# Stacking 85 inner rows in two weight tiles, direct copies across halves, and gram moves issued by GpSimd

## The reference, cut to what matters

```python
# N_DENSE 13, N_FIELDS 26, VOCAB 6250, K 64, batch 512, HID = 325 + 26*64 + 13 = 2002
sparse_embed = emb_tables[field_idx[None, :], x_sparse]          # 512 x 26 x 64, gathered rows
z = sparse_embed.reshape(B, N_FIELDS * K)
gram = jnp.einsum('bik,bjk->bij', sparse_embed, sparse_embed)
inner = gram[:, iu, ju]                                          # the 325 pairs i < j
dnn_in = jnp.concatenate([x_dense, z, inner], axis=-1)           # 512 x 2002
h = jax.nn.relu(dnn_in @ w1 + b1)                                # w1 is 2002 x 2002
out = jax.nn.sigmoid(h @ w2 + b2)
```

## Time and profile before

| | |
|---|---|
| median of 3 runs | 210.6 us (209.88 to 210.68) |
| profiled execution, its own time | 210.68 us |
| its span, first to last instruction | 208.6 us |
| PE busy | 200.1 us (96%) |
| DVE, ACT, POOL busy | 145.3, 130.2, 121.2 us |
| moved by DMA | 38.99 MB, 187 GB/s on average |

### The profile page before, as it was taken

One profiled execution on the slowest core, in us unless ns is written; L12 is line 12 of the kernel. 1 busy time (PEld: TensorE's weight loads), 2 busy tenths in 40 slices (PEclk: granted clock), 3 DMA queues, 4 the chain that ended last, 5 costly groups with the idle time before them and its releaser, 6 DMA issues.

```text
span 208.6 us, 3830 instructions
## 1 busy us (share of the span) xinstructions
PE 200.1 (96%) x1340; PEld 163.9 (79%) x1340; DVE 145.3 (70%) x341; ACT 130.2 (62%) x262; POOL 121.2 (58%) x162
## 2 busy tenths in 40 slices
PE   8999989989999969999999999999999999999993
PEld 8966868868888848878888888888888888788882
DVE  3656829088879289678587989557498896673473
ACT  2755437089989578889367663868689957542201
POOL 4878777778777781446898898889883000000000
PEclk9999999999999996999999999999999999999999
DMA  5389958788785922266787648768868385023100
GB/s 152 95 268 290 306 219 279 300 281 282 257 262 187 291 55 23 102 154 161 217 281 229 205 119 294 247 217 257 292 209 231 91 279 212 3 46 55 32 0 0
DMA packets 15387, 38.99 MB, mean 187 GB/s; under 512 B 3881, under 2 KB 5281, under 8 KB 15369
## 3 DMA queue, kind: packets, MB, share of 16 engines
q1 hardware_dynamic: 11688, 35.27, 52.1%
q0 software_dynamic: 3328, 3.41, 7.2%
q10 hardware_dynamic: 353, 0.08, 0.2%
HBM read 37.71 MB, written 0.69 MB: 184 GB/s over the span
## 4 chain that ended last, share of the span: by engine, by line
PE 60%; POOL 21%; issue 7%; DMA 6%; ACT 2%; DVE 2%; DVEq 0%
POOL E L825 21%; PE slot L1083 17%; PE slot L1086 16%; PE slot L1089 16%; DMA E<-emb,row_idx 6%; PE slot L1043 5%; PE slot L1074 2%; PE slot L1073 2%; PE slot L1075 2%; ACT ET L882 2%; DMA x_idx<-idx 1%; DVE G L981 1%; DVE slot L1007 1%; DVE T L950 0%; ACT parked L887 0%
## 5 line engine op out<-in xcount | busy, mean ns | idle before, releaser
L825 POOL DMA_INDIRECT E<-emb,row_idx x104 | 111.5, 1072 | 36.9 <-issue 23.2
L933 DVE TENSOR_TENSOR w_lo<-w_raw,w_hi 128x500 fp32r<-128x500 f32 (+6 forms) x128 | 79.6, 672 | 5.2 <-ACT w_hi L851 4.8
L1083 PE MATMUL slot<-w_hi,x_hi 128*128 128x500 f32 (+5 forms) x236 | 74.8, 398 | 1.8 <-ACT x_hi L877 1.8
L851 ACT CAST w_hi<-w_raw 128x1000 fp32r<-128x1000 f32 (+6 forms) x64 | 64.5, 1028 | 16.3 <-DMA w_raw<-w 12.2
L1086 PE MATMUL slot<-w_lo,x_hi 128*128 128x500 f32 (+5 forms) x236 | 73.0, 391 | 0.0
L1089 PE MATMUL slot<-w_hi,x_lo 128*128 128x500 f32 (+5 forms) x236 | 72.7, 389 | 0.0
L1083 PEld LDWEIGHTS slot<-w_hi,x_hi 128*128 128x128 f32 (+2 forms) x236 | 43.9, 190 | 11.8 <-ACT x_hi L877 2.7
L1086 PEld LDWEIGHTS slot<-w_lo,x_hi 128*128 128x128 f32 (+2 forms) x236 | 44.8, 190 | 9.2
L1089 PEld LDWEIGHTS slot<-w_hi,x_lo 128*128 128x128 f32 (+2 forms) x236 | 44.5, 189 | 9.3
L882 ACT COPY ET<-T 32x128 f32<-32x128 f32 (+4 forms) x91 | 33.1, 364 | 2.2
L950 DVE STREAM_TRANSPOSE T<-E 128x256 f32<-128x256 f32 x24 | 10.6, 444 | 33.4 <-DMA E<-emb,row_idx 33.3
(11 more groups left out here) (39 smaller groups left out, 80.4 us busy)
## 6 DMA issues: line engine op xcount, KB each, us to landing
w_raw<-w SPq DMA_DIRECT2D x32, 501.0 KB, 4.5
w_raw<-w SPq DMA_DIRECT2D x32, 500.0 KB, 4.8
E<-emb,row_idx POOLq DMA_INDIRECT x104, 3.7
w_all<-w SPq DMA_DIRECT2D x1, 1001.0 KB, 6.8
gram_dram<-G SPq DMA_DIRECT2D x8, 84.5 KB
x_in<-gram_dram SPq DMA_DIRECT2D x8, 42.0 KB
x_in<-G SPq DMA_DIRECT2D x4, 58.5 KB
x_in<-G SPq DMA_DIRECT2D x4, 19.5 KB
```

The source lines that it names most:

```text
L825: nc.gpsimd.indirect_dma_start(out=E[:, k % ER, j, :], out_offset=None, in_=emb_rows, in_offset=bass.IndirectOffsetOnAxis(ap=row_idx[:, at ...
L851: nc.scalar.copy(w_parts(m)[0], w_source(m)).then_inc(w_hi_ready, 1)
L933: nc.vector.tensor_tensor(lo[:, cols], w_source(m)[:, cols], hi[:, cols].bitcast(F32), ALU.subtract)\
L1083: nc.tensor.matmul(acc[q], xh, hi[:, cols[q]], start=first, stop=False)
```

## The change

It has four inner tiles for three (`IT` = 4, `NT` = 17, so 68 pieces for 64). 85 of the inner rows (`BOTH`: 78 pairs and 7 dense features) stand in the two tiles `TERMS_A` and `TERMS_B`. In `TERMS_A` these rows hold the rest of the weight and the rounded input, in `TERMS_B` the rounded weight and the rest of the input; their hi times hi stands in the remaining rows of both tiles. A step of such a tile is one pass of two matmuls. The other inner rows stand in `FULL_0` and `FULL_1` with three passes. So the inner tiles cost 1 + 1 + 3 + 3 = 8 passes. Doubled pairs and their zero rows are gone: the fetches take rectangles.

The moves of a block become 10 DMAs: four copies and two stores in the "store", four reads in the "fetch". SP keeps those of `bt` 2. POOL issues those of `bt` 0 and 1 between its gathers (`BY_POOL`) and those of `bt` 3 behind its last gather. The planner doesn't book POOL's time for them. `make_todo` puts two inner steps for one ahead, the tiles of B1 group 5 ahead of B2 group 2, and the gram rounds of `bt` 2 and 3 earlier. SP loads the dense features (three DMAs in place of one on ACT). `ones`, `wrap` and two index tiles share the space of `G`, `x_lo` has 15 places.

```diff
+IT = 4
 NT = ZT + IT
+TERMS_A, TERMS_B, FULL_0, FULL_1 = range(ZT, NT)
+BOTH = 6 * HALF + 7
+CROSS_AT = [(TERMS_A, 0, 0, 6), (TERMS_A, BOTH + 3, 0, 3), (TERMS_B, BOTH + 4, 3, 6), (FULL_0, 0, 6, HALF)]
...
+BY_SYNC = 2
+BY_POOL = {56: ("store", 0), 58: ("fetch", 0), 60: ("store", 1), 61: ("fetch", 1)}
...
-    todo += q5[:1] + mixed(gram({1}), q5[1:] + inner_0[:1], per=2)
+    todo += q5[:1] + mixed(gram({1}), q5[1:] + inner_0[:2], per=2)
     later = [inner("A", 1, 0), inner("A", 0, 1), inner("A", 1, 1)]
-    todo += inner_0[1:] + [s for steps in later for s in steps[:1]] + [s for steps in later for s in steps[1:]]
+    todo += inner_0[2:] + later[0] + [s for steps in later[1:] for s in steps[:2]]
+    todo += [s for steps in later[1:] for s in steps[2:]]
...
     for n, g in enumerate(GROUP_ORDER[2:]):
         todo += b_group("B1", 1, g)
-        todo += b_group("B2", 0, GROUP_ORDER[n]) if n < 4 else []
-    rest = [s for g in GROUP_ORDER[4:] for s in b_group("B2", 0, g)]
-    todo += mixed(rest[:7], gram({2, 3}), every=2) + rest[7:]
+        todo += b_group("B2", 0, GROUP_ORDER[n]) if n < 3 else []
+    rest = [s for g in GROUP_ORDER[3:] for s in b_group("B2", 0, g)]
+    todo += rest[:1] + mixed(rest[1:9], gram({2, 3}), every=2) + rest[9:]
     later = [inner("B1", 1, 2), inner("B1", 1, 3), inner("B2", 0, 2), inner("B2", 0, 3)]
-    todo += [s for steps in later for s in steps[:1]] + [s for steps in later for s in steps[1:]]
+    todo += [s for steps in later for s in steps[:2]] + [s for steps in later for s in steps[2:]]
...
+TERMS_LEN = 0.46
+INNER_LAND = (3.8, 4.6, 9.0, 10.0)
...
-                    if m >= RAW:
-                        sp.wait_ge(w_split, 2 * (m - RAW + 1))
+                    if m >= RAW and PIECES[USED[m - RAW]][1] == TERMS_B:
+                        sp.wait_ge(w_hi_ready, w_hi_count(m - RAW))
+                    elif m >= RAW:
+                        sp.wait_ge(w_split, w_split_count(m - RAW, 1))
...
+            def move(part, bt):
+                if part == "store":
+                    pool.wait_ge(g_copied_act, evac_count("act", rounds_of(bt)))
+                    pool.wait_ge(g_copied_dve, evac_count("dve", rounds_of(bt)))
+                    for n, (m, to, src) in enumerate(cross_moves(bt)):
+                        pool.dma_start(to, src).then_inc(x_in_landed[bt][m], 16)
+                        if n == 0:
+                            for u in (0, 1):
+                                pool.dma_start(*within_store(bt, u)).then_inc(g_stored[bt], 16)
+                if part == "fetch":
+                    pool.wait_ge(g_stored[bt], 32)
+                    for m, to, src in within_fetches(bt):
+                        pool.dma_start(to, src).then_inc(x_in_landed[bt][m], 16)
...
                 for j in range(GROUP_GATHERS[g]):
+                    if at in BY_POOL:
+                        move(*BY_POOL[at])
                     nc.gpsimd.indirect_dma_start(
...
+            move("store", BT - 1)
+            move("fetch", BT - 1)
...
+                    if t in (TERMS_A, TERMS_B):
+                        if t == TERMS_A:
+                            pe.wait_ge(x_hi_ready, x_hi_count(*key_of(step)))
+                        else:
+                            pe.wait_ge(x_split, x_lo_count(*key_of(step)))
+                            pe.wait_ge(w_hi_ready, w_hi_count(RANK[n]))
+                        for q in (0, 1):
+                            if t == TERMS_A:
+                                pe.wait_ge(w_split, w_split_count(RANK[n], q))
+                            last = nc.tensor.matmul(acc[q], xh, hi[:, cols[q]], start=first, stop=end)
```

More of the change, by code:

```diff
@@ L179, in cell_at, with pe_len @@
     return cell_of(step[2], t, h)
+def pe_len(step):
+    if step[0] == "product" and piece_of(step)[1] in (TERMS_A, TERMS_B):
+        return TERMS_LEN
+    return PE_LEN[step[0]]
 def gate_of(m):
@@ L192, in part_of, with shelf, earlier @@
     return next(p for p, (a, b) in enumerate(ET_PARTS) if a <= g < b)
+def shelf(pieces, m):
+    return m - sum(PIECES[n][1] == TERMS_B for n in pieces[:m + 1])
+def earlier(pieces, m):
+    return [n for k, n in enumerate(pieces[:m]) if shelf(pieces, k) == shelf(pieces, m) - HL]
 INNER_KEYS = [IN_KEY + m for m in range(IT)]
 PE_LEN = {"product": 1.38, "gram": 1.15}
+TERMS_LEN = 0.46
 ACT_LEN = {"hi": 1.05, "x24": 0.55, "x_hi": 0.43, "evac": 0.36, "park": 0.62}
@@ L325, in update @@
                 if m >= RAW:
-                    if ("lo", m - RAW, 1) not in done:
+                    last = ("hi", m - RAW) if PIECES[pieces[m - RAW]][1] == TERMS_B else ("lo", m - RAW, 1)
+                    if last not in done:
                         break
-                    at = max(at, done["lo", m - RAW, 1] + HOP)
+                    at = max(at, done[last] + HOP)
                 load(m, max(at, w_landed[-1] - 2.0))
         while next_hi < len(w_landed):
[L331 to L335, removed]
+            free = all_done([("p",) + s for n in earlier(pieces, next_hi) for s in uses[n]])
+            if free is None:
+                break
             offer_once("act", ("hi", next_hi), max(w_landed[next_hi], free + HOP))
@@ L358, in update @@
                                 offer_once(engine, op, max(done["gram", n], moved) + HOP)
+        for bt in range(BT):
             at = all_done([op for n in gram_rounds(bt) for op in evac_ops(n, bt)])
             if at is not None and ("moved", bt) not in done:
-                at = max(at, done.get(("moved", bt - 1), 0.0) - 5.0)
-                done["moved", bt] = at + 8.8
-                sp_events.append((at + HOP, ("store", bt)))
-                sp_events.append((at + 4.0, ("fetch", bt)))
-                for m, later in enumerate((3.4, 8.4, 8.6)):
+                if bt == BY_SYNC:
+                    sp_events.append((at + HOP, ("store", bt)))
+                    sp_events.append((at + 4.0, ("fetch", bt)))
+                done["moved", bt] = at + INNER_LAND[-1]
+                for m, later in enumerate(INNER_LAND):
                     offer_once("act", ("x_hi", bt, IN_KEY + m), at + later)
@@ L487, in run @@
             done[op] = end
-            offer("dve", ("x_lo",) + op[1:], end + HOP)
+            if op[2] not in (KEY_A, KEY_B):
+                offer("dve", ("x_lo",) + op[1:], end + HOP)
+            elif ("x_hi", op[1], KEY_A) in done and ("x_hi", op[1], KEY_B) in done:
+                offer("dve", ("x_lo", op[1], KEY_B), end + HOP)
         elif kind == "hi":
             done[op] = end
-            for q in (0, 1):
+            for q in (0, 1) if PIECES[pieces[op[1]]][1] != TERMS_B else ():
                 offer("dve", ("lo", op[1], q), end + HOP + 0.01 * q)
@@ L516, in make_orders @@
             orders["pe"].append(best)
-            end = clock["pe"] + PE_LEN[best[0]]
+            end = clock["pe"] + pe_len(best)
             clock["pe"] = end
@@ L699, in w_parts @@
             ph, t, h = PIECES[USED[m]]
-            return (w_hi[0:KROWS[t], m % HL, 0:HALF_W[h]], w_lo[0:KROWS[t], m % HL, 0:HALF_W[h]])
+            hi, lo = [w[0:KROWS[t], shelf(USED, m) % HL, 0:HALF_W[h]] for w in (w_hi, w_lo)]
+            return (lo, None) if t == TERMS_B else (hi, lo)
         def x_group(bt, g):
@@ L848, in _ @@
                     act.wait_ge(w_landed[m % RAW], 16 * (m // RAW + 1))
[L849 to L850 removed]
+                    for n in earlier(USED, m):
+                        act.wait_ge(piece_done, released_count(n))
                     nc.scalar.copy(w_parts(m)[0], w_source(m)).then_inc(w_hi_ready, 1)
@@ L922, in _ @@
             nc.vector.memset(parts[:], 0.0).then_inc(parts_ready, 1)
-            nc.vector.memset(x_in[96:ONES_AT + 1, :, IT - 1, :], 1.0).then_inc(ones_row_ready, 1)
+            nc.vector.memset(x_in[64:96, :, TERMS_B - ZT, :], 0.0).then_inc(pads_ready, 1)
+            nc.vector.memset(x_in[ONES_ROW[1]:ONES_ROW[1] + 1, :, ONES_ROW[0] - ZT, :], 1.0).then_inc(pads_ready, 1)
             landed = [0] * ER
```

162 lines of the change are left out of this document (96 added, 66 removed).

## The result

The changed kernel takes 225.33 us (median of 4 runs, 223.67 to 225.65); the kernel before, run beside it, 210.24. The ratio is 1.0737 (95% interval 1.0681 to 1.0794). I had predicted 217.0, in a range of 208 to 225: the side was right, the size was not, and the result lies just outside the range. The profiled execution took 225.65 us, its span is 223.4.

The account below looks back on a forecast made before the run. PE was taken as the bound from 78.4 us on, with POOL's gathers close behind: 210.68 - 0.7 (saved passes and step order at bt 3 group 5) + 7.0 (gathers' delay) = 217.0 us, range 208 to 225.

Parts of the forecast that it names:

- The price of a DMA on POOL: Time a plain DMA takes of POOL between gathers: 0.5 us taken, between bounds of 0.16 and 1.25.
- The delay D = 7.0: On POOL, gather 61 starts at 103.6 us where it started at 96.66, and all gathers behind are as late.
- the 103.6 of the prediction: Forecast start in us of gather 61 on POOL, behind 20 plain DMAs; before the change 96.66.
- 1.34 us a gather: Average time of a gather with its memset on POOL, taken from 85.96 to 91.17 us as holding four.
- Nothing lets them catch up: POOL's gathers behind number 61 stay as late as it is; the only gaps are the 0.16 us of issue.
- rival 1: PE stays the bound, 207.0 to 209.6 us; gathers 61 to 103 avoid collisions and recover 7 us; chance 0.17.
- Two of four steps lie behind: At group 5 of bt 3, pulled-ahead steps leave two of four behind: end 0.7 us less than before, plus delay.
- What the gram moves themselves do at the end is covered: After gram round 7, seven product steps (9.6 us) cover the moves of bt 2 and 3; no added time.
- In phase A a late `x_in` costs PE time, but it is the same delay: A late x_in only uses up time PE would wait for at the gathers; nothing added.
- At nothing: The 2 MB more of loads, 8.4 us of DMA at 238 GB/s, are hidden; 4.2 us if uncovered.
- The gain: PE saves one pass for 4 blocks x 2 halves: 8 x 0.456 = 3.65 us.
- c: Price of one plain DMA on POOL, taken as 0.5 us; 0.3 to 0.9 gives 213 to 225 us.

Follow-up runs that it names:

- run 3: The changed kernel with the moves of bt 0 and 1 given back to SP, those of bt 3 left on POOL: 214.27 us, ratio 1.018.
- run 6: The changed kernel with POOL's moves booked in the planner and the landings of bt 0 and 1 set to match: 225.53 us, ratio 1.0793.
- run 4: The kernel before with 20 spare DMAs added on POOL, its own moves still on SP, planner not told: 221.61 us, ratio 1.0527.
- run 11: The kernel before with the hi times lo pass of the last inner tile left out, output incomplete: ratio 0.9895, 2.2 us less.
- run 9: The kernel before with the memsets after gathers taken away, which also changes the planner's booked gather times: 214.94 us, ratio 1.0231.
- runs 8: The version of run 6 with the memsets after gathers taken away, which also changes the planner's booked gather times: 220.12 us, too spread to compare.

## Why the prediction was wrong

**The price of a DMA on POOL.** "I take 0.5": it is 0.61, with a mean that hardly varies (0.67 and 0.69 for the first of a row, 0.55 for those of a store within a half). 20 x 0.11 = 2.2 us. By the Trainium skill, "SBUF — State Buffer", section "SBUF: two separate sides", such a DMA takes about 620 ns alone; the time that one holds POOL in this trace is near that (0.61), though the section doesn't say which part of a DMA it means. Its 3,100 ns beside a DVE copy no run here shows. The rule of the Trainium skill, "DMA: Bandwidth & Descriptors", section "Issuing engine by pattern", to leave plain copies to Sync, came out right for bt 0 and 1: after and run 3 set its worth here at 11 us.

**The delay D = 7.0**, where the trace has 14.1. Beside the 2.2 the store of bt 0 began at 90.14 and not 86.85, 3.3. None of that is POOL's DMAs, since the first of them is this one: PE had come to that gram round late, behind its wait at 75.92 and a low clock, and in the stacked versions this start lies between 84.6 and 90.2, for 85.9 to 87.2 in those with the layout of before; each of four gathers behind DMAs begins after 0.30 us and not 0.16, 0.6 together; gather 60 took 1.96, 0.9 more than its like. Together 7.0, of the 7.2 between 110.79 and the 103.6 of the prediction. (Its 1.34 us a gather counts the gap behind the fourth one; 85.96 to 91.17 alone gives 1.30, 0.2 us less over five gathers.) "Nothing lets them catch up" held but for 2.5 us: 42 gathers at 1.39 us for 1.45. That is the effect of rival 1, at a third of its size; whether by fewer collisions is not shown.

**"Two of four steps lie behind"** gave -0.7; three did, one was pulled ahead: +0.7.

**"What the gram moves themselves do at the end is covered"** was wrong, by 2.0 us. I had put the landing of the first tile at what one copy takes. The first tile now needs two copies, the second behind both stores, and SP and POOL issue at the same time. SP's part of after:

```profile
195.17 0.83 SPq L867 DMA_DIRECT2D x_in<-G  x1
196.05 2.16 SPq L870 DMA_DIRECT2D gram_dram<-G  x2
198.26 4.43 SPq L867 DMA_DIRECT2D x_in<-G  x3
```

and ACT's cast of TERMS_A, 9.0 us after the store began, where before it was 3.4 (183.76 to 187.16):

```profile
204.13 1.26 ACT L954 CAST x_hi<-x_in 127x128 fp32r<-127x128 f32 x4 [5.91 <-DMA x_in<-G]
```

**"In phase A a late `x_in` costs PE time, but it is the same delay"** is neither shown nor refuted for this kernel: in run 6 5.1 us of low clock went and the time stayed, but the waits for moved pairs stayed, too. The waits are elsewhere than I put them: 1.5 us for gathered tiles at the later groups where I expected some 10, 8.3 at moved pairs, with a low clock behind the early ones. In run 4, without the planner's booking, 5.7 us were lost just there: a late gather at the head of ACT's and DVE's lists holds casts that are ready.

**"At nothing" for the extra loads.** By themselves they cost nothing that shows; with SP issuing ten DMAs a block the weight behind the moves was late in run 3. The kernel that I costed, with SP freed and POOL paying, is not the one where this decides, but by the account of run 3 it is part of why the layout without POOL's DMAs lost too.

**The gain** of 3.65 us was sized as PE's pace, which held (110.53, 110.99, 111.44: 0.456 a pass). On the path a pass was worth 2.2 (1.2 to 3.3, run 11).

So the side came from the right mechanism, plain DMAs on POOL ahead of the gathers. That the 20 of bt 0 and 1 cost about 11 of the 15 us is shown twice, by taking them off (run 3) and by putting like ones on the kernel before (run 4). That the gathers' delay is the main way is read from the traces; run 4 shows a second one, through SP's moves. The sum, put right: 217.0 + 4.6 (last gather 11.6 late and not 7.0) + 1.4 (order) + 2.0 (end) = 225.0, for 225.65. Most of it is in D, where I gave the whole uncertainty to c and none to the start of the store and to what follows each DMA. Open stay: why the start of the store moves by up to 5.6 us among the stacked versions, how much of the loss the waits for moved pairs at the inner steps would make by themselves, and what made run 9 slower.

## What to carry to other kernels

Price a saved matmul pass only after every DMA that its layout adds has an issuing engine and a place in that engine's order: here ten issues a block at 0.5 to 1.0 us each stood against a pass that is worth some 2 us in all, and no version, with the moves on SP, on ACT or on POOL, came back to the time before. When work is delayed on one engine, look at the head of every in-order list that waits for it, not only at the tile that uses it last. A constant that a planner reads, too, changes more than the instruction that it names (runs 8 and 9). A tile that is put together from several copies is ready with the last one, behind all that the same queue issues between them.

## What the runs showed of the hardware that I had not expected

- A DMA on POOL costs the next gather, too: the gap ahead of a gather is 0.30 us behind another DMA and 0.16 behind a memset. A memset of 0.17 us between gathers is therefore nearly free (1.28 against 1.25 us a gather).
- SP issues copies out of `G` more slowly while another queue does so: three take 2.4 us alone, 4.0 beside ACT's and 5.8 beside POOL's. ACT's are slowed, too (3.5 for 2.4), POOL's are not (1.9 either way).
- Waits of 2 to 3 us were followed by a granted clock of 0.58 to 0.74 for five to ten microseconds (run 3, and 0.63 and 0.69 in after from 115 to 125 us), but not each time: in run 6 waits of 2.7, 1.7 and 1.1 us stand between 100 and 115 us, and every stretch up to 125 us has 1.00. What decides it is not shown.
